# The second layer norm of a transformer block moved from ScalarE to VectorE, and the steps behind it one slot up, on one Trainium2 core

## The reference

```
x = x + layernorm(attention(layernorm(x)))
x = x + layernorm(ffn(layernorm(x)))

layernorm(x) = (x - mean(x)) / sqrt(var(x) + 1e-5)
```

## Time and profile before

| | before |
|---|---|
| median of 3 runs | 1507.53 us (1507.41 to 1508.8) |
| the profiled execution, its own time | 1508.8 us |
| its span in the trace | 1507.1 us |
| TensorE busy | 1468.6 us, 97% |
| VectorE busy | 997.0 us, 66% |
| ScalarE busy | 680.4 us, 45% |
| GpSimd busy | 453.7 us, 30% |

### The profile page before, as it was taken

How to read it: one execution, slowest core, us unless ns; L and a number is a source line. 1 busy time by engine, 2 the same in 40 slices (tenths; PEclk the granted TensorE clock), 3 DMA queues, 4 the chain that set the end, 5 groups by cost and what they waited for, 6 DMA issues and landing times. The chain is left out here.

```text
span 1507.1 us, 37448 instructions
## 1 busy us (share of the span) xinstructions
PE 1468.6 (97%) x14436; PEld 1280.9 (85%) x14436; DVE 997.0 (66%) x2388; ACT 680.4 (45%) x1261; POOL 453.7 (30%) x720
## 2 busy tenths in 40 slices
PE   7799999999999999999999999999999999999997
PEld 6678888888888888888888888888888888888886
DVE  4646766666676766766666676766766666776765
ACT  4543544445344453545445344453535445344433
POOL 1422512234141332512234141332513234141231
PEclk9999999999999999999999999999999999999999
DMA  3300000000000000000000000000000000000000
GB/s 113 112 1 2 21 7 14 14 14 14 0 14 14 14 14 0 21 7 14 14 14 14 0 14 14 14 14 0 25 3 14 14 14 14 0 14 16 2 8 22
DMA packets 25345, 24.59 MB, mean 16 GB/s; under 512 B 2016, under 2 KB 25056, under 8 KB 25312
## 3 DMA queue, kind: packets, MB, share of 16 engines
q1 hardware_dynamic: 25312, 24.13, 5.0%
HBM read 15.74 MB, written 8.39 MB: 16 GB/s over the span
## 5 line engine op out<-in xcount | busy, mean ns | idle before, releaser
L677 ACT ACTIVATE h_hi<-late 128x512 fp32r<-128x512 f32 x256 | 161.6, 631 | 271.7 <-DVE late L956 271.5
L956 DVE TENSOR_TENSOR late<-late,up_ps 128x512 f32<-128x512 f32 x256 | 175.4, 685 | 158.0 <-PE up_ps L422 100.6
L422 PE MATMUL down_ps<-w_hi,h_hi 128*128 128x256 f32 x976 | 264.5, 293 | 0.0
L422 PE MATMUL down_ps<-w_hi,h_lo 128*128 128x256 f32 x976 | 253.9, 282 | 0.0
L758 ACT ACTIVATE late<-gate_ps 128x512 f32<-128x512 f32 x256 | 151.9, 593 | 220.9 <-PE gate_ps L422 216.3
L1164 POOL TENSOR_TENSOR rms_in<-rms_in,minus_half 128x16 f32<-128x16 f32 x32 | 93.8, 2930 | 510.7 <-DVE rms_in L920 510.7
L978 DVE SCALAR_TENSOR_TENSOR late<-down_ps,route,late 128x256 f32<-128x256 f32 x364 | 158.6, 477 | 105.6 <-PE down_ps L422 102.7
L871 DVE TENSOR_TENSOR h_lo<-late,h_hi 128x512 fp32r<-128x512 f32 x256 | 175.5, 685 | 64.7 <-ACT h_hi L677 64.7
L422 PE MATMUL gate_ps<-ft_hi,w_hi 128*128 128x512 f32 x512 | 204.3, 399 | 0.7 <-ACT ft_hi L677 0.4
L422 PE MATMUL gate_ps<-ft_hi,w_lo 128*128 128x512 f32 x512 | 203.0, 397 | 0.0
L422 PE MATMUL up_ps<-ft_hi,w_hi 128*128 128x512 f32 x512 | 199.3, 389 | 0.0
(11 more groups left out here) (161 smaller groups left out, 2571.6 us busy)
## 6 DMA issues: line engine op xcount, KB each, us to landing
xs<-in_x SPq DMA_DIRECT2D x32, 256.0 KB, 2.9
out_rows<-late SPq DMA_DIRECT2D x32, 256.0 KB, 2.2
late<-in_wg SPq DMA_DIRECT2D x8, 256.0 KB, 3.3
late<-in_wu SPq DMA_DIRECT2D x8, 256.0 KB, 2.7
late<-in_wd SPq DMA_DIRECT2D x8, 256.0 KB, 3.0
late<-in_wkv_t SPq DMA_DIRECT2D x1, 512.0 KB, 5.4
late<-in_wq_t SPq DMA_DIRECT2D x1, 256.0 KB, 4.6
late<-in_wo_t SPq DMA_DIRECT2D x1, 256.0 KB, 4.7
```

What stands on the lines that cost most here:

```text
L422: last = nc.tensor.matmul(dst, lhs, rhs, start=n == 0, stop=n == len(terms + low_terms) - 1)
L677: return nc.scalar.activation(dst, src, ACT.Copy)
L956: nc.vector.tensor_tensor(h_f[:, m, :], h_f[:, m, :], up_ps[m][:, :], ALU.mult).then_inc(h_ready[0], 1)
```

## The change

Norm 2 leaves ScalarE. In `ln2_stats` VectorE, once its moments are there, subtracts the mean from the pair's rows in place (two `tensor_scalar`), while GpSimd takes the root of variance plus epsilon with two instructions. The step `ln2_apply` and `shift2` are gone. `ln2_add` is now two `scalar_tensor_tensor`, `rows * rstd + xs` into `x1`. In `STEPS` the add and statistics of pair 1 go from slot 23 to slot 22, and `ln3_apply` 0 and 1 from slots 24 and 25 to 23 and 24. In `FIRST_STEPS` only `ln2_apply` is taken out.

```
     [("wo", 0), ("ot", 1)],
     [("ln2_stats", 0)],
-    [("wo", 1), ("ln2_apply", 0)],
+    [("wo", 1)],
     [("ln2_stats", 1), ("ln2_add", 0), ("ln3_stats", 0)],
-    [],
-    [("ln2_apply", 1), ("ln2_add", 1), ("ln3_stats", 1)],
+    [("ln2_add", 1), ("ln3_stats", 1)],
     [("ln3_apply", 0)],
     [("ln3_apply", 1)],
+    [],
     [("ft", 0), ("ft", 1), ("ft_out", 0), ("ft_out", 1)],
...
# ScalarE
-                elif kind == "ln2_apply":
-                    p = step[1]
-                    ln_apply(2, p + 1, a, rows, rows, range(2 * p, 2 * p + 2), shift2, rstd2).then_inc(ln2_applied[0], 1)
...
# VectorE
                     reach(dve, wo_copied, a, p + 1)
                     ln_stats(2, rows, range(2 * p, 2 * p + 2), bn2, mv2)
+                    reach(dve, moments_ready[1], a, p + 1)
+
+                    for t in range(2 * p, 2 * p + 2):
+                        last = nc.vector.tensor_scalar(rows[:, t, :], rows[:, t, :], mv2[:, t, 0:1], None, ALU.subtract)
+                    last.then_inc(centred[0], 1)
                 elif kind == "ln2_add":
                     p = step[1]
-                    ts = slice(2 * p, 2 * p + 2)
-                    reach(dve, ln2_applied, a, p + 1)
+                    reach(dve, rstd_ready[1], a, p + 1)
+                    reach(dve, centred, a, p + 1)
                     reach(dve, x1_copied, a, 0)
-                    nc.vector.tensor_tensor(x1[:, ts, :], rows[:, ts, :], xs[:, ts, :], ALU.add).then_inc(x1_ready[0], 1)
+                    for t in range(2 * p, 2 * p + 2):
+                        last = nc.vector.scalar_tensor_tensor(x1[:, t, :], rows[:, t, :], rstd2[:, t:t + 1], xs[:, t, :],
+                                                              ALU.mult, ALU.add)
+                    last.then_inc(x1_ready[0], 1)
...
# GpSimd
                 if kind == "ln2_stats":
                     p = step[1]
-                    inverse_root(2, p + 1, slice(2 * p, 2 * p + 2), a, mv2, var2, rstd2, shift2)
+                    ts = slice(2 * p, 2 * p + 2)
+                    reach(pool, moments_ready[1], a, p + 1)
+                    settle(nc.gpsimd.tensor_tensor(var2[:, ts], mv2[:, ts, 1], ln_eps[:, ts], ALU.add))
+                    nc.gpsimd.tensor_tensor(rstd2[:, ts], var2[:, ts], minus_half[:, 0, ts], ALU.pow).then_inc(rstd_ready[1][0], 1)
```

## The result

| | before | changed |
|---|---|---|
| median | 1507.47 us (4 runs, 1507.39 to 1508.8) | 1551.37 us (4 runs, 1548.48 to 1557.14) |
| ratio, 95% interval | | 1.0294 [1.026, 1.0328] |
| profiled execution | 1508.8 us | 1553.75 us |

The change makes the kernel 2.9% slower. The forecast was 1542 us with a range of 1526 to 1556, so the time lies inside the range.

What follows compares the result with a forecast made beforehand. TensorE, busy 97% of the span, was taken as the bound. 15 x (2.69 - 0.53) = 32.4 us, less 1.7 first block, plus 4 clock, gave 34.7 us: 1542 us predicted against 1507.53, range 1526 to 1556.

Steps and rivals of the forecast that it cites:

- rival B: Same pause before down(6, 0), but the clock falls in more than a third of blocks: +40 to +59 us; 22%.
- A: Wait of 2.4 to 3.0 us before down(6, 0), clock dropping in at most a third of blocks: +26 to +43 us; 60%.
- a sign of being wrong in size: Wrong in size if the scalar_tensor_tensor pair is nearer to 0.74 us, or the clock falls in most blocks.
- the slack of 0.38 us at `down(6, 0)`: Half 1's h_lo ends at 244.16, down(6, 0) starts at 244.54; VectorE has no idle time from 240.96 to catch up.
- The work put ahead of `h_lo`, 2.92 us: On VectorE: 0.70 centring, 0.21 dearer add of pair 0, 2.01 for pair 1's moved add and statistics.
- The new wait, 2.69 us a block: TensorE's down(6, 0) starts at 247.23 in place of 244.54, waiting for h_lo; 2.4 to 3.0 us allowed.
- The gain before `ft`, 0.53: Pair 1's rows are ready before TensorE reaches the ft transposes, saving 0.53 us a block.
- The first block, 1.7: In the first block, which runs alone, the step through ScalarE goes: 1.7 us gained.
- The centring priced by the row and not by the page: VectorE's tensor_scalar priced at the trace's 348 ns; the Trainium skill's page would make the sum some 5 us smaller.
- The clock: Pauses sometimes halve TensorE's clock, 1.5 us a stretch: 4 us for two to three of fifteen blocks, 24 for all.
- What else the profile was to show: First-block ft 1 near 66.3, ScalarE about 35 us less busy, VectorE about 24 us more.

Runs made afterwards that it cites:

- order-alone run: The kernel before, norm still on ScalarE, with pair 1's apply, add and statistics moved to slot 22 and ln3_apply to 23 and 24: 1548.06 us, 1.0262.
- the run with the steps moved back: The changed kernel, norm on VectorE, with pair 1's add and statistics back in slot 23 and ln3_apply in 24 and 25: 1516.29 us, 1.0053.
- the filled pause: The changed kernel with nine unused matmuls into up_ps[1] ahead of down(6, 0) in the loop blocks: 1539.08 us, 1.02.

## Why the prediction was right, and where it was off

The pause was forecast at the right place and of the right size, and that is 32 of the 44 us. The number, though, came out by rival B, which had 22%, and not by A, the forecast, which had 60%: 43.9 us is just above A's upper end, and the clock fell in ten blocks and not in at most five. The prediction named that itself as a sign of being wrong in size. That the time still lies in the range is owed to the lower half of B, which the range took in.

- *What bounds the kernel, and the slack of 0.38 us at `down(6, 0)`:* right. TensorE's new wait is there, 15 times, at that place, and VectorE has no hole ahead of it. The order-alone run and the run with the steps moved back show that the order is the cause of most of it, not the norm's work.
- *The work put ahead of `h_lo`, 2.92 us:* measured 2.85. L937 has the row's 348 ns price (0.64 for two), and it starts 0.04 us after the moments are there (242.01 to 242.05), the lower of the two waits that I had. The pair of L945 took 0.87 to 0.88 us, the value that I took, not the 0.74 of the lower bound.
- *The new wait, 2.69 us a block:* 2.60, and 0.10 more in `down(6, 0)` behind it, which the sum did not have. *The gain before `ft`, 0.53:* 0.55. Together 15 x (2.69 - 0.53) = 32.4 us were forecast, and 39.0 + 1.5 - 8.3 = 32.2 measured.
- *The first block, 1.7:* 2.06, but that agreement is in part chance: the change's own part up to `ft` 1 is 2.23, and the clock took 0.70 and gave 0.53 in these two executions.
- *The centring priced by the row and not by the page:* L937 runs at the price of L966. The Trainium skill ("VectorE: DVE Perf Modes", Mode 2x_2P) would have had it at twice the speed of the two-input form. The trace's 0.64 us for the pair stands against 0.74 for two of those, so the measurement decides against it at this size.
- *The clock:* the term that was mis-sized. I booked 4 us, two to three stretches at 1.2 GHz of fifteen, and gave 60% to at most a third. The profiled execution has ten, 14.9 us, and a median run about eight; the price of one, 1.5, was right (1.3 to 1.6, and by it all fifteen are 22.5 us, not 24). The step that failed was the count: of the two pauses that it went by, one was followed by the halved clock, and from no row two to three of fifteen were made of that; half of fifteen would have been seven or eight. How often a pause of this length halves the clock was open, and two pauses of one execution could not tell. Without this term the sum is 1539.5, and the filled pause measured 1539.08.
- *What else the profile was to show:* `ft` 1 near 66.3 (66.50), ScalarE 35 us less busy (29.9: L683 had overlapped its neighbours by about 0.1 us each), VectorE 24 more (27.9).

## What to carry to other kernels

Where an engine runs several lists of work in one fixed order, ask of a step that moves up what it moves past, and how long before its use that is ready: here 0.38 us of slack against 2.9 us of work. Such a step is cheap only where its engine waits anyway: with the work of pair 0 in a hole of 2.1 us, and that of pair 1 behind the `h_lo` again, 2.9% slower became 0.7% faster. A pause of the bounding TensorE can cost a second time through its clock, so look at the granted clock around each new wait.

## What was not expected of the hardware

Pauses of 2.44 us in an otherwise dense stream of matmuls were followed by a stretch at 1.2 GHz in ten of fifteen blocks, the rest of them not, with identical instructions around them; pauses of 2.3 us (the order alone) in five of fifteen, pauses of 1.3 us in none. In the first block the pause of 1.87 us near 43 us left the clock at 1.00 in the kernel before, while over 44 to 46 us it was 0.50 in the run of the order alone, whose instructions up to there are the same. From one execution of the changed kernel to another the time varied by 8.7 us (1548.48 to 1557.14), and the mean granted clock was 0.982 in the slowest and 0.987 and 0.989 in the two fastest; the kernel whose pauses are filled varied by 1.2 us (1538.1 to 1539.32). What decides in which blocks the clock falls was not tried.
